# Attention reordered per batch, with 1024-column cosine pieces in one PSUM ring, clip and square in place

## The reference

```python
q, k, v = heads(layernorm(x) @ w_qkv.T + b_qkv)         # q and k scaled to length 1
cos = einsum('bhsd,bhtd->bhst', q, k)
g_dist = arccos(clip(cos, -1 + 1e-7, 1 - 1e-7))
attn_score = (1 + g_dist) ** (-3.2)
n_r = attn_score.sum(-1); n_c = attn_score.sum(-2)
k_tilde = attn_score / n_r[..., :, None] / n_c[..., None, :]
out = (k_tilde / k_tilde.sum(-1, keepdims=True)) @ v      # then @ w_out.T + b_out, + x
x = x + u + top-2 of 16 experts on u + 2 shared experts / 2     # u = layernorm(x)
```

## Time and profile before

| | us |
|---|---|
| runs before, median (3 runs) | 5460.44 (5460.04 to 5466.84) |
| the profiled execution, first to last instruction (its span) | 5470.8 |
| first whole logarithm L1150 (batch 0) | 279.91 |
| last one (batch 63) | 5102.93 |
| start of the third stage | 5154.05 |

### The profile page before, as it was taken

One profiled execution on the slowest core, in us unless ns is written; L12 is line 12 of the kernel. 1 busy time (PEld: TensorE's weight loads), 2 busy tenths in 40 slices (PEclk: granted clock), 3 DMA queues, 4 the chain that ended last, 5 costly groups with the idle time before them and its releaser, 6 DMA issues. The chain is left out here.

```text
span 5470.8 us, 46435 instructions
## 1 busy us (share of the span) xinstructions
PE 3563.2 (65%) x10518; PEld 930.7 (17%) x10678; DVE 3866.7 (71%) x6677; ACT 4928.6 (90%) x2159; POOL 1820.8 (33%) x545
## 2 busy tenths in 40 slices
PE   8655556555566555565557666676766667676599
PEld 4211111111111111111111111111211111121244
DVE  7766667666677666676678777777777677776466
ACT  5699999999999999999999998989999998999521
POOL 0133333333343433343433333334243333333000
PEclk9666666666566666666657666676666766676799
DMA  2100000000000000000000001010100101010200
GB/s 85 62 8 14 18 18 10 13 18 17 17 17 12 12 10 10 10 7 5 12 28 31 28 26 35 14 39 10 49 11 23 35 25 33 3 50 2 80 25 19
DMA packets 71895, 128.58 MB, mean 24 GB/s; under 512 B 9654, under 2 KB 46937, under 8 KB 71706
## 3 DMA queue, kind: packets, MB, share of 16 engines
q1 hardware_dynamic: 70554, 122.50, 7.1%
q0 software_dynamic: 1152, 4.19, 0.3%
HBM read 96.77 MB, written 29.88 MB: 23 GB/s over the span
## 5 line engine op out<-in xcount | busy, mean ns | idle before, releaser
L786 PE MATMUL psum<-stacks 128*128 128x512 bf16 x3936 | 2081.3, 553 | 1677.3 <-DVE cosc L917 1368.2
L1110 POOL TENSOR_TENSOR X<-cosc 128x2048 f32<-128x2048 f32 x504 | 1812.4, 3607 | 3108.2 <-DVE cosc L917 1948.4
L917 DVE TENSOR_SCALAR cosc<-psum 128x512 f32<-128x512 f32 x2048 | 1291.9, 683 | 320.3 <-PE psum L786 197.7
L929 DVE TENSOR_TENSOR X<-psum,X 128x512 f32<-128x512 f32 x2048 | 1328.8, 687 | 115.7 <-ACT X L1138 24.4
L1142 ACT ACTIVATE X<-X 128x4096 f32<-128x4096 f32 (+1 forms) x192 | 905.7, 4749 | 159.4 <-DVE X L929 159.4
L786 PEld LDWEIGHTS psum<-stacks 128*128 128x128 bf16 x4096 | 398.4, 103 | 3570.0 <-DVE cosc L917 2003.4
L1153 ACT ACTIVATE X<-X 128x2048 f32<-128x2048 f32 x512 | 970.0, 1895 | 2.0
L1138 ACT ACTIVATE X<-X 128x4096 f32<-128x4096 f32 (+1 forms) x320 | 910.8, 2921 | 0.7
L1150 ACT ACTIVATE X<-X,consts 128x16384 f32<-128x16384 f32 x64 | 892.7, 13949 | 0.8
L1134 ACT ACTIVATE X<-X,consts 128x16384 f32<-128x16384 f32 x64 | 891.9, 13936 | 0.0
L809 PE MATMUL psum<-X,vp 128*32 128x512 f32 x4096 | 719.8, 836 | 17.5 <-DVE vp L939 17.5
(11 more groups left out here) (165 smaller groups left out, 1230.2 us busy)
## 6 DMA issues: line engine op xcount, KB each, us to landing
V<-expert_w SPq DMA_DIRECT2D x64, 512.0 KB, 3.6
stacks<-qk_parts SPq DMA_DIRECT2D x256, 64.0 KB
qk_parts<-X SPq DMA_DIRECT2D x96, 128.0 KB, 1.9
stacks<-qk_parts SPq DMA_DIRECT2D x64, 192.0 KB
head_out<-evac SPq DMA_DIRECT2D x32, 256.0 KB, 2.1
expert_w<-u_t SPq DMA_DIRECT2D x17, 256.0 KB, 2.6
X<-in_L_attn_x_dram POOLq DMA_DIRECT2D x8, 512.0 KB, 4.2
stacks<-qk_parts SPq DMA_DIRECT2D x32, 128.0 KB
```

The lines of the kernel that those rows point to most:

```text
L786: return nc.tensor.matmul(dst, stacks[:, 1, buf, keys:keys + P], stacks[:, 0, buf, q0:q0 + n], start=True, stop=True)
L917: nc.vector.tensor_scalar(cosc[:, i % 2, j * 512:(j + 1) * 512], ps_clip[j % 2], -CLIP, CLIP, ALU.max, ALU.min).then_inc(clip_ok, 1)
L929: nc.vector.tensor_tensor(part, ps_mult[j % 2], part, ALU.mult).then_inc(mult_ok, 1)
L1110: nc.gpsimd.tensor_tensor(X[:, m % 2, i, :], cosc[:, i % 2, :], cosc[:, i % 2, :], ALU.mult).then_inc(square_ok, 1)
```

## The change

The cosine pieces become 1024 columns wide (two matmuls into two neighbouring banks, one signal), and clips and products share one ring of two such pieces, `ps_cos`, with one pair of counters, `cos_ps` and `cos_ok`. `cosc` is gone: VectorE clips into `X` in place of the tile and GpSimd squares there. For that the clip, and no longer the square, waits for the column sums of the batch two before. The order of a period becomes: VectorE values of batch n (two groups of four tiles), eight products of batch n+1, the copy of the sums, eight clips of batch n+2, then weights or side work. TensorE: product tile 0, eight additions, product tiles 1 to 7, eight clips, the rest. ScalarE's first logarithm comes in two pieces, the sigmoids in four; the exponentials signal once for four tiles. `vp` holds eight tiles, and a group's value rows are made by one reciprocal and one product. Before the first period nothing is interleaved.

```diff
-        ps_clip = banks[1:3]
-        ps_mult = banks[3:5]
+        CW = 1024
+        PER = S // CW
+        ps_cos = [psum[:, 1 + 2 * b:3 + 2 * b, :].rearrange("p a b -> p (a b)") for b in range(2)]
-        BEFORE, AFTER = (4, 5), (6, 7)
-        RECIP_STARTS = (0, 1, 2, 4, 6)
+        LOG_PIECES = ((0, 4), (4, 8))
+        HALF_PIECES = ((0, 2), (2, 4), (4, 6), (6, 8))
+        ATAN_PIECES = ((0, 4), (4, 6), (6, 8))
+        EXP_PIECES = ((0, 4), (4, 8))
...
 # TensorE
+                def pieces(m, i, first):
+                    for j in range(PER):
+                        wait(pe, cos_ok, first + j - 1)
+                        for q in range(0, CW, 512):
+                            mm = cosines(ps_cos[j % 2][:, q:q + 512], m, i, j * CW + q, 512)
+                        mm.then_inc(cos_ps, 1)
...
                 def emit(k, m, beside):
-                    for i in range(BT // 2):
-                        if has(k, m + 2):
-                            clip(k, m + 2, i)
-                        add(k, m, 2 * i)
-                        add(k, m, 2 * i + 1)
-                    if has(k, m + 2):
-                        for i in BEFORE:
-                            clip(k, m + 2, i)
                     if has(k, m + 1):
-                        for i in range(BT):
+                        mult(k, m + 1, 0)
+                    for i in range(BT):
+                        add(k, m, i)
+                    if has(k, m + 1):
+                        for i in range(1, BT):
                             mult(k, m + 1, i)
                     if has(k, m + 2):
-                        for i in AFTER:
+                        for i in range(BT):
                             clip(k, m + 2, i)
...
 # VectorE
                 def clip(k, m, i):
-                    wait(dve, square_ok, t - 1)
-                    for j in range(4):
-                        dve.wait_ge(clip_ps, t * 4 + j + 1)
-                        nc.vector.tensor_scalar(cosc[:, i % 2, j * 512:(j + 1) * 512], ps_clip[j % 2],
-                                                -CLIP, CLIP, ALU.max, ALU.min).then_inc(clip_ok, 1)
+                    wait(dve, sum_ps, (n - 2) * BT + i + 1)
+                    for j in range(PER):
+                        dve.wait_ge(cos_ps, first + j + 1)
+                        nc.vector.tensor_scalar(X[:, m % 2, i, j * CW:(j + 1) * CW], ps_cos[j % 2],
+                                                -CLIP, CLIP, ALU.max, ALU.min).then_inc(cos_ok, 1)
...
+                def values(k, m, piece):
+                    a, b = EXP_PIECES[piece]
+                    dve.wait_ge(score_ok, n * len(EXP_PIECES) + piece + 1)
+                    wait(dve, sum_ps, (n - 1) * BT + b)
+                    nc.vector.reciprocal(vp[:, a:b, HD:HD + 1].rearrange("p t o -> p (t o)"), ncol[:, a:b]).then_inc(nc_ok, 1)
...
+                    nc.vector.tensor_tensor(vp[:, a:b, 0:HD],
...
                 def emit(k, m, beside):
-                    for i in range(BT // 2):
-                        values(k, m, 2 * i)
-                        values(k, m, 2 * i + 1)
-                        if has(k, m + 2):
-                            clip(k, m + 2, i)
-                    if has(k, m + 2):
-                        for i in BEFORE:
-                            clip(k, m + 2, i)
+                    for piece in range(len(EXP_PIECES)):
+                        values(k, m, piece)
                     if has(k, m + 1):
                         for i in range(BT):
                             mult(k, m + 1, i)
-                    if beside == "tail" and isinstance(k, int) and k == SIDE and m == 0:
-                        side_scales()
-                    if has(k, m + 2):
-                        for i in AFTER:
-                            clip(k, m + 2, i)
                     if m % 2 == 1:
...
                         nc.vector.tensor_copy(evac[:, :], ps_sum).then_inc(sum_ok, 1)
+                    if has(k, m + 2):
+                        for i in range(BT):
+                            clip(k, m + 2, i)
...
 # GpSimd
-                    pool.wait_ge(clip_ok, t * 4 + 4)
-                    wait(pool, sum_ps, t - 2 * BT + 1)
-                    nc.gpsimd.tensor_tensor(X[:, m % 2, i, :], cosc[:, i % 2, :], cosc[:, i % 2, :],
-                                            ALU.mult).then_inc(square_ok, 1)
+                    pool.wait_ge(cos_ok, clips(4 * k + m, i))
+                    own = X[:, m % 2, i, :]
+                    nc.gpsimd.tensor_tensor(own, own, own, ALU.mult).then_inc(square_ok, 1)
...
 # ScalarE
+                    for a, b in LOG_PIECES:
+                        act.wait_ge(square_ok, n * BT + b)
+                        own = tiles(m, a, b)
+                        nc.scalar.activation(own, own, ACT.Ln, bias=one_c, scale=-1.0).then_inc(log_ok, 1)
...
+                    act.wait_ge(log2_ok, n + 1)
+                    for piece, (a, b) in enumerate(EXP_PIECES):
+                        wait(act, vp_ok, n * len(EXP_PIECES))
+                        for i in range(a, b):
+                            own = X[:, m % 2, i, :]
+                            last = nc.scalar.activation(own, own, ACT.Exp, scale=POWER, accum_out=ncol[:, i:i + 1])
+                        last.then_inc(score_ok, 1)
```

More of the change, by code:

```diff
@@ L644, in pre_ln_arccos_attention_moe_kernel, with clips, mults @@
         t_in = sem("t_in")
-        BEFORE, AFTER = (4, 5), (6, 7)
-        RECIP_STARTS = (0, 1, 2, 4, 6)
+        LOG_PIECES = ((0, 4), (4, 8))
+        HALF_PIECES = ((0, 2), (2, 4), (4, 6), (6, 8))
+        ATAN_PIECES = ((0, 4), (4, 6), (6, 8))
+        EXP_PIECES = ((0, 4), (4, 8))
+        def clips(n, i):
+            if isinstance(n, int) and n == 1:
+                return PER * (BT + i + 1)
+            return n * 2 * BT * PER + PER * (i + 1)
+        def mults(n, i):
+            if isinstance(n, int) and n == 0:
+                return PER * (2 * BT + i + 1)
+            return n * 2 * BT * PER + PER * (BT + i + 1)
         WEIGHTS = 1 + NR // 4
@@ L808, in add @@
                     for j in range(4):
-                        mm = nc.tensor.matmul(ps_sum[32 * j:32 * j + 32, :], vp[:, i % 4, :],
+                        mm = nc.tensor.matmul(ps_sum[32 * j:32 * j + 32, :], vp[:, i, :],
                                               X[:, m % 2, i, j * 512:(j + 1) * 512],
@@ L861, in side_work, with weights @@
                         mm.then_inc(side_g_ps, 1)
-                        side_chunks(k, 0, CH2)
                     if m == 3:
                         pe.wait_ge(side_gt, t2 + 1)
-                        side_chunks(k, CH2, NC)
+                def weights(k, m):
+                    if isinstance(k, int) and k == 0:
+                        pe.wait_ge(en_sum, 1)
+                    else:
+                        pe.wait_ge(en_in, (expert(k, m) + 2) * 16)
+                    for kc in range(KC):
+                        for oc in range(KC):
+                            mm = nc.tensor.transpose(ps_misc[:, (kc * KC + oc) * P:(kc * KC + oc + 1) * P],
+                                                     e_nat[:, oc, kc * P:(kc + 1) * P], ident[:, :])
+                    mm.then_inc(et_ps, 1)
                 def emit(k, m, beside):
@@ L931, in values @@
[L931 to L942 removed]
+                    n = 4 * k + m
@@ new lines, in clip @@
+                    first = clips(n, i) - PER
+                    wait(dve, sum_ps, (n - 2) * BT + i + 1)
[3 more added lines that the diff above has]
+                                                -CLIP, CLIP, ALU.max, ALU.min).then_inc(cos_ok, 1)
+                def mult(k, m, i):
+                    n = 4 * k + m
+                    first = mults(n, i) - PER
+                    for piece, (a, b) in enumerate(HALF_PIECES):
+                        if i == a:
+                            dve.wait_ge(half_ok, n * len(HALF_PIECES) + piece + 1)
+                    for j in range(PER):
+                        dve.wait_ge(cos_ps, first + j + 1)
+                        part = X[:, m % 2, i, j * CW:(j + 1) * CW]
+                        nc.vector.tensor_tensor(part, ps_cos[j % 2], part, ALU.mult).then_inc(cos_ok, 1)
@@ L1047, in side_work, with weights @@
                         side_choose(k)
-                        side_gather(k, 0, CH2)
-                    if m == 3:
-                        side_gather(k, CH2, NC)
-                def emit(k, m, beside):
-                    for i in range(BT // 2):
-                        values(k, m, 2 * i)
-                        values(k, m, 2 * i + 1)
-                        if has(k, m + 2):
-                            clip(k, m + 2, i)
-                    if has(k, m + 2):
-                        for i in BEFORE:
-                            clip(k, m + 2, i)
+                def weights(k, m):
+                    shared = isinstance(k, int) and k == 0
+                    if shared:
+                        dve.wait_ge(en_in, 32)
```

(21 more changed lines are left out.)

128 lines of the change are left out of this document (45 added, 83 removed).

## The result

| | before | after | forecast |
|---|---|---|---|
| median of the runs on one chip, us | 5462.24 (5460.04 to 5466.84, 4 runs) | 5337.47 (5336.1 to 5340.28, 4 runs) | 5324, 5278 to 5390 |
| ratio, 95% interval | | 0.9768 (0.9754 to 0.9782) | |
| span of the profiled execution, us | 5470.8 | 5335.6 | 5334 |

What follows compares the result with a forecast made beforehand. ScalarE's own work was taken to bound the attention. Start -9.7, the 63 batches -129.7 and end +3 gave -136 us, a span of 5334; less 10.4 for the profiled execution, 5324 us, range 5278 to 5390.

Steps and rivals of the forecast that it cites:

- What bounds it: Attention: ScalarE's own work sets the time; product waits total 159.4 us; a batch outside the tail comes to 73.97 us.
- the logarithm's extra piece and the lost sigmoid piece: ScalarE's list: one logarithm piece more and one sigmoid piece fewer, each put at 0.07 us, so they cancel.
- The pace: Products on VectorE and TensorE: 1024-column operation 1.22 us, one piece every 1.17, 18.8 us for 16 against 22.2.
- Rival C: Product pieces no cheaper than two old ones, 1.39 us; 1.2 to 1.3 us per batch return, 5406; chance 0.09.
- Squares and clips: VectorE's clips end at +85.7 and GpSimd's squares at +97.9 (+23.9 of the next batch), with 12 us of cover.
- The cover of 5.1 us a tile: GpSimd's squares in place, 3.57 us a tile, cost nothing as long as each stays below 5.1 us.
- The tail: Second half of the batches, with expert side work: all ScalarE gaps left there taken as 29 us, bounds 5 and 90.
- the side exponential: Tail, ScalarE after batch 1 of four: side chain ends near +29.5 against +29.1, a 0.4 us gap, eight times.
- the full clock: TensorE's eight additions in the tail taken at 7.7 us, after dense matmuls, instead of 14.6 at the low clock.
- B: Tail additions at the low clock and chains catching more squares: 8 x 6.9 us more, 5380; chance 0.17.
- Start and end: First whole logarithm at 270.2 us instead of 279.9; four additions after the last exponential instead of one, +3 us.
- The sum: Whole kernel: -9.7 - 129.7 + 3 = -136 us against the profiled 5470.8, a span of 5334.
- the step I added last: From span to time: 10.4 us taken off because the profiled execution lay above the runs' median, giving 5324.

Runs made afterwards that it cites:

- e11: Changed kernel with the tail's side work ahead of the clips, plus first logarithm in one piece and sigmoids in three: 5348.46 us (0.9793).
- e12: Changed kernel with tail side work ahead of the clips, sigmoids in three pieces, first logarithm whole only outside the tail: 5299.31 us (0.9694).
- e3: Kernel before the change, with only clips 4 and 5 of the next batch moved behind the products: 5435.27 us (0.995).
- e9: Changed kernel with 512-column pieces in two single banks and product tile 0 behind the additions in TensorE's order: 5494.54 us (1.0061).
- e10: Changed kernel with product tile 0 behind the additions in TensorE's order, 1024-column pieces kept: 5353.29 us (0.9803).
- e8: Changed kernel with an extra half square per tile on GpSimd, into a spare buffer, ahead of each square: 5580.2 us (1.0213).
- e1: Changed kernel with 512-column pieces in a ring of two single banks, product tile 0 still ahead of the additions: 5925.61 us (1.0845).
- e7: Changed kernel with the exponentials' accumulator output left out and the values divided by ones: 5303.97 us (0.9703).
- e2: Changed kernel with 512-column pieces in a ring of four single banks: 5344.46 us (0.9782).

## Why the prediction held, step by step

- **What bounds it.** Right. ScalarE's own list sets the time and the product wait was the only thing to win. Both gaps outside the tail are gone. The interval was forecast at 73.97 and is 74.05: I let the logarithm's extra piece and the lost sigmoid piece cancel at 0.07 each, but two logarithm pieces take 14.12 instead of 13.94 (+0.18) and four sigmoid pieces 14.14 instead of 14.23 (-0.09). Times 63 that is 5.7 us, the largest mis-sized term. e11 and e12 confirm it from the other side: 73.77 us a batch outside the tail with both undone. Two smaller errors hide behind it and cancel by luck. The interval of 73.97 that the forecast took as one without a gap holds a small side function of ScalarE (0.1 us); e3 shows the old list without it, 73.86. And the first exponential now starts 14.08 us behind its logarithm's start instead of 13.98; why, no run shows.
- **The pace.** Operation 1.22 forecast, 1.218 measured; pace 1.17 forecast, 1.18 in the median batch, where TensorE is at the lower level and the round binds as worked out (1.18), and 1.13 to 1.15 where it is at the higher one and VectorE binds, as was worked out too. Products were to run from +48.1 to +66.9 and run from +48.5 to +67.3 in the median. Rival C (1.39) is excluded. e9 shows what an unchanged pace costs, and that the prediction's way of computing a round (operation, matmul and hand-overs over two buffers) is right. C's price was too low, though: it counted 1.3 us a batch and came to 5406, and e9, whose products end as late, takes 5494, since each gap of the tail grows too (16 us of it are product tile 0's place, by e10).
- **Squares and clips.** Clips to +85.7, measured +85.5 in the batch shown and +86.6 in one at the lower level; squares to +97.9, measured +98.3 (1477.95 - 1379.68). The cover of 5.1 us a tile was measured by e8 as 5.05.
- **The tail.** Gaps of 29 us forecast, 26.5 measured: 17.7 once (18.5), 6.1 at the side exponential in 8 (3.2), 2.7 in 4 at the products (7 in 8). These misses of 3 and 4 us nearly cancel, which is luck. Four held operations a chain, as forecast (of 16 in the chain of the choice, not 17), and in the batch at 3177.76 the path came as worked out: the chain from +11.8 to +26.3, the gathering's end at +43.3, product tile 1 at +51.9 for 52.5. That 0.6 us, and a pace of 1.14 behind it, is why no gap follows. The additions took 7.1 us in each of the seven batches where they stand between a first gathering and products (granted clock 1.00 in the one shown), so the full clock was the right choice and B (14.6) did not come. What I did not see is that this hangs on product tile 0 ahead of the additions: e10 gives 16 us without it.
- **Start and end.** 270.2 forecast, 269.37 measured; +3 at the end, +2.6 measured.
- **The sum.** Span 5334 forecast, 5335.6 measured, with +5.7 at the intervals, -2.5 at the gaps and -1.9 at the start and the end. Of the 13 us between the forecast time and the median, 10.4 are the step I added last: I carried over that the profiled execution of before lay 10.4 us above its runs. The span of after lies 1.9 below its median. One execution's distance from the median of three runs says nothing of another kernel: the kernel before ran from 5450 to 5474 us in the rounds of the experiments. The forecast time would have been nearer without that step; the forecast span, 1.6 us off, owes some of its closeness to these terms of opposite sign.

By the Trainium skill (SBUF — State Buffer, the section on its two sides), a VectorE operation with two SBUF inputs or in a two-port mode and a GpSimd operation that reads SBUF take turns for whole instructions. The trace agrees: small operations of these kinds took up to 3.53 us in the squares' stretch and 0.19 outside it, the small reductions and reciprocals between them kept 0.17 to 0.19 inside it, and 1024-column clips from PSUM kept 1.22 us beside unbroken squares.

Left open: how the 97 us of the tail divide between the order that clipping in place allows, grouped value rows (in e3 two of the eight value operations ahead of the products shown took 3.56 us each instead of 0.23) and the faster round. No run changes one of them alone against e3.

## What to carry to other kernels

Write the consumer's wanted times beside the producer's times for one period, and put each piece of work where it has most cover; here clips with 12 us of cover stood ahead of products with none. Work that is placed ahead of a wait in a queue must fit in the ring whole, or it turns from a reserve (16 us, e10 against the changed kernel) into a block (431 us, e1 against e9). Cover can be spent only once: after each move, measure again what is left before cutting pieces elsewhere.

## What the runs showed of the hardware

- A read of ScalarE's accumulator lasts 0.186 us in the rows but costs 0.094 us of time (e7): the next exponential starts before it ends.
- An extra piece of a ScalarE function over the same data cost 0.18 us for the logarithm (14.12 against 13.94) and 0.09 for the sigmoid (14.23 against 14.14).
- With TensorE at a granted 0.50, 512-column operations of VectorE from PSUM follow each other at 0.69 us over two single banks (e9) and at 0.60 over four (e2), and those of 1024 columns at 1.18 over two pairs of banks. At 1.00 the two single banks give 0.60 too (e1; the eight clips of the earlier trace rows), and the two pairs 1.13. Four banks keep the pace at or near VectorE's own in either form and at either level; two are enough at the higher one alone.
- Half a square on GpSimd took 1.89 us where a whole one takes 3.60 (e8), so the time goes nearly with the columns.
